# SyncE's queue in the last FFN part of a six-block decoder: stores of products wait for the load in flight

## What is computed

```python
x = act_qdq(x)
up = act_qdq(x @ lpbq_dequant(w_up).T)        # 256 -> 768
gate = act_qdq(x @ lpbq_dequant(w_gate).T)
sig = fixed_qdq_u16(jax.nn.sigmoid(gate))
gate = act_qdq(gate * sig)
o = act_qdq(gate * up)
return o @ lpbq_dequant(w_down).T             # 768 -> 256
```

## Time and profile before

| | us |
|---|---|
| median of 3 runs | 1373.13 |
| lowest, highest | 1371.76, 1376.19 |
| span of the profiled execution | 1374.7 |

### The profile page before, as it was taken

The page is one execution under the profiler, slowest core; times in us unless marked ns, Lnnn a source line. Parts: engine busy times, 40 slices in busy tenths (PEclk is TensorE's granted clock), DMA queues, the critical chain, the costliest instruction groups (busy, mean ns, idle before and its releaser), DMA issues.

```text
span 1374.7 us, 18473 instructions
## 1 busy us (share of the span) xinstructions
PE 1243.7 (90%) x7340; PEld 828.6 (60%) x7340; DVE 1048.2 (76%) x1966; ACT 517.7 (38%) x608; POOL 267.8 (19%) x194
## 2 busy tenths in 40 slices
PE   7899999997999999853779999999999999998976
PEld 4566666665644554321566776767768686766654
DVE  3578899986634789998564787969878797887777
ACT  1244334433534567587013323232322333231421
POOL 0011111112100000033100413204132141413242
PEclk9899999999999999976899999999999999999998
DMA  5001000102582045489322011100211000000000
GB/s 219 16 16 32 31 1 31 32 16 93 150 295 77 31 153 185 167 315 373 107 87 84 31 54 62 54 31 32 63 54 54 32 24 21 27 20 36 1 16 16
DMA packets 47829, 107.86 MB, mean 78 GB/s; under 512 B 10752, under 2 KB 31360, under 8 KB 44288
## 3 DMA queue, kind: packets, MB, share of 16 engines
q1 hardware_dynamic: 43584, 104.59, 21.7%
q10 hardware_dynamic: 4160, 2.10, 0.5%
HBM read 62.64 MB, written 44.04 MB: 78 GB/s over the span
## 4 chain that ended last, share of the span: by engine, by line
PE 74%; DVE 16%; DMA 3%; ACT 3%; issue 2%; POOL 1%; SPq 0%; POOLq 0%; ACTq 0%; DVEq 0%
PE ps L1357 8%; PE ps L1420 7%; PE ps L1236 6%; PE ps L1067 6%; PE ps L1118 4%; PE ps L817 4%; PE ps L1393 3%; PE ps L1302 3%; PE ps L965 2%; PE ps L890 2%; PE ps L1326 2%; PE ps L1337 2%; PE ps L1467 2%; DMA arena<-up_scratch 2%; PE ps L908 2%
## 5 line engine op out<-in xcount | busy, mean ns | idle before, releaser
L1420 PE MATMUL ps<-arena 128*128 128x256 f32 x512 | 120.1, 389 | 5.8 <-ACT arena L1892 5.8
L1357 PE MATMUL ps<-arena 128*128 128x512 f32 x256 | 117.6, 598 | 0.0
L1420 PEld LDWEIGHTS ps<-arena 128*128 128x128 f32 x512 | 98.6, 195 | 27.9 <-ACT arena L1892 9.9
L2535 DVE TENSOR_TENSOR arena<-ps,arena 128x2048 f32<-128x2048 f32 x32 | 73.3, 2292 | 38.1 <-PE ps L1302 37.9
L1938 POOL TENSOR_TENSOR arena<-arena 128x4 f32<-128x4 f32 x44 | 45.5, 1038 | 282.0 <-DVE arena L2124 282.0
L1998 POOL TENSOR_TENSOR arena<-arena 128x16 f32<-128x16 f32 x32 | 92.2, 2916 | 32.5 <-DVE arena L2564 32.5
L1236 PE MATMUL ps<-arena 128*128 128x256 f32 x384 | 88.2, 386 | 5.2 <-DVE arena L2456 5.2
L1067 PE MATMUL ps<-arena 128*128 128x512 f32 x192 | 83.8, 593 | 1.2 <-ACT arena L1620 1.2
L1118 PE MATMUL ps<-arena 128*128 128x512 f32 x192 | 84.4, 594 | 0.0
L1236 PEld LDWEIGHTS ps<-arena 128*128 128x128 f32 x384 | 73.0, 194 | 16.5 <-issue 7.0
L1357 PEld LDWEIGHTS ps<-arena 128*128 128x128 f32 x256 | 46.2, 190 | 48.7 <-issue 45.1
(11 more groups left out here) (311 smaller groups left out, 2651.9 us busy)
## 6 DMA issues: line engine op xcount, KB each, us to landing
v_scratch<-arena SPq DMA_DIRECT2D x7, 1536.0 KB, 12.9
arena<-v_scratch SPq DMA_DIRECT2D x7, 1536.0 KB, 6.8
up_scratch<-arena SPq DMA_DIRECT2D x6, 1536.0 KB, 6.0
arena<-up_scratch SPq DMA_DIRECT2D x6, 1536.0 KB, 12.6
vw_scratch<-arena SPq DMA_DIRECT2D x32, 256.0 KB, 3.8
arena<-x_scratch SPq DMA_DIRECT2D x16, 512.0 KB, 4.7
arena<-vw_scratch SPq DMA_DIRECT2D x8, 1024.0 KB
arena<-x SPq DMA_DIRECT2D x8, 512.0 KB, 5.7
```

Source lines behind the costliest of these rows:

```text
L1357: last = mm(flat(p % 2), w["cos_wq"][:, k, p * P:(p + 1) * P], xt4[:, k], start=k == 0, stop=k == NC - 1)
L1420: last = mm(flat(2)[:, C:2 * C], cos_pt[:, p], cos_vw[:, par, p], start=p == 0, stop=p == NP - 1)
L2535: v.tensor_tensor(met_s[:, n % 2].rearrange("p r t h n -> p (r t h) n"), flat(3, 4).rearrange("p (h n) -> p h n", n=P), w["causal"].unsque ...
```

## The change

A new helper on SP waits until the load of batch q has landed. It is put ahead of the stores of products 0 to 4. `load_up(4)` now stands ahead of `store_v(1)`, and `store_vw(15)` ahead of `store_v(2)`. No engine computes anything else or in another order, and the transfers are the same in number and size.

```diff
+            def up_landed(q):
+                wait_moved(sp, "up_loaded", Batch(q), q % 2, 2)
+
             load_up(2)
             store_vw(13)
             load_up(3)
+            up_landed(3)
             store_v(0)
             store_vw(14)
+            load_up(4)
+            up_landed(4)
             store_v(1)
-            load_up(4)
             load_up(5)
+            store_vw(15)
+            up_landed(5)
             store_v(2)
-            store_vw(15)
             load_up(6)
+            up_landed(6)
             store_v(3)
             load_up(7)
+            up_landed(7)
             store_v(4)
             store_v(5)
             store_v(6)
```

## The result

| | median, us | lowest, highest | runs |
|---|---|---|---|
| before | 1372.62 | 1369.85, 1377.73 | 19 |
| changed | 1378.11 | 1375.36, 1381.27 | 19 |

The changed kernel is slower. The ratio to before is 1.0033, with a 95% interval of 1.0022 to 1.0044, which is 3.0 to 6.0 us. The forecast was + 2.8 us and a time of 1375.9 within 1371.0 to 1381.0. The direction was right, and the time is in the range, but the size was a half to two thirds of what was measured. The outcome lies on the edge between "within 0.3%", to which I gave 0.68, and "slower by over 0.3%", to which I gave 0.29. The ratios in this document leave out three later runs of the kernel before, at 1494 to 2589 us.

What follows compares the result with a forecast made beforehand. Transfers, DVE and ACT were taken as nearly full, with the chain through load 6. Gaps at the gates, partly filled, and an earlier load 3 put load 6 2.8 us later: 1373.13 + 2.8 = 1375.9 us, range 1371.0 to 1381.0.

Steps and rivals of the forecast that it cites:

- What bounds, and the chain: From 600 to 630 us transfers, DVE and ACT are nearly full; the waits run through loads 4 and 6.
- The gates bind, and the queue runs dry: At SP's new waits, stores are held until a load lands and the queue empties, adding 2.4 us at loads 3 to 5.
- The landing of load 6: On SP's queue, load 6 lands at 632.6 us in place of 629.8, 2.8 us later.
- The two plain rounds: From load 4 to load 5 and on to load 6: a store and a load by bytes plus 2.4 us, 10.4 each.
- the first term: Issue of load 2 to landing of load 3: 9.3 us of bytes plus 2.4 us, landing at 600.1.
- The round with side store 14: From load 3 to load 4, with stores 0 and 14 ahead of load 4, which lands at 611.8 us.
- The long-gap rival: At the gates each restart of the queue costs 3.8 us, as the first did; + 4.1 to + 8.4 us, chance 0.25.
- The short gaps: At the gates the queue restarts in under 2.0 us; - 3.7 to + 1.2 us, chance 0.20.
- The estimate by the Trainium skill: On SP's queue, 2.0 us fixed per transfer and 436 GB/s put load 6 at 627.7 us and the time at 1371.0.
- ACT and load 4: On ACT, the 2.07 us wait for load 4 goes, since ACT is free at 612.6 us and the load has landed.
- From load 6 to the scale: ACT's 9.3 us of work follows load 6, DVE idles some 6 us, and the scale is ready at 660.3, 2.8 later.
- The tail: Store 6 lands at 661.3 us, 1.0 behind the scale, just covered; as rival setting the end, 1379.7 us, chance 0.04.

Runs made afterwards that it cites:

- covered gates: The changed kernel's order without the gate at load 3, the next load issued ahead of each gate at loads 4 to 7; ratio to before 0.9989.
- second run: The changed kernel run once more, with nothing altered; ratio to the kernel before 1.0034.
- gates 3 to 5: The changed kernel without the gates at loads 6 and 7; ratio to the kernel before 1.0046.
- gate 3 alone: The changed kernel's order of transfers with only the gate at load 3; ratio to the kernel before 1.0021.
- the two experiments: Changed kernel with side store 14 ahead of the gate at load 3, ratio 1.0032; and with side stores 13 to 15 at a quarter of their rows, 1.0023.
- the order without gates: The changed kernel with its new order of transfers on SP but without the five gates; ratio to the kernel before 0.9996.

## Why the prediction was right in direction and short in size

**What bounds, and the chain.** Right. The chain went through load 6, and with gates 6 and 7 away nothing changed, so what is behind load 6 wasn't on it.

**The gates bind, and the queue runs dry.** Right: stores of products were issued at 598.2, 611.7, 622.4, 632.6 and 642.9, and the covered gates show that it is the dry queue that costs.

**The landing of load 6** was put 44.2 us after the issue of load 2 (632.6 - 588.4) and came after 46.8 and 46.4. By its terms, with what the profiles of the changed kernel, its second run, gates 3 to 5 and (up to load 4) gate 3 alone measured:

| term | forecast | measured |
|---|---|---|
| issue of load 2 to landing of load 3 | 11.7 | 12.4, 13.3, 13.0, 13.4 |
| load 3 to load 4 | 11.7 | 13.6, 12.2, 12.2, 13.5 |
| load 4 to load 5 | 10.4 | 10.6, 10.8, 10.5 |
| load 5 to load 6 | 10.4 | 10.2, 10.1, 10.9 |

The two plain rounds of a store and a load were right: 4.0 + 4.0 + 2.4, against 10.5 on average. (That the 2.4 are there whatever the size isn't borne out: the 128 KB stores of y have 1.4. The sum uses it for 1536 KB only.) The step that failed is the first term. I had taken the 3.8 us over the bytes of load 3 for an effect of store 0 behind it, and forecast 2.4 once that store was held back, a gain of 1.4. With the gate, load 3 landed after 13.0 us on average. In the six lists in which store 0 followed it at once it landed after 12.6 to 14.5 us, 13.5 on average (13.1 in the kernel before, from which I had worked). So the gain was about 0.4, inside the spread of either group, in place of 1.4, and load 3 came 1.3 us later than forecast. What the 3.7 us over its bytes are stays open.

The round with side store 14 was short by 1.2 more, of which the two experiments explain a part. Slices of the changed kernel show a part too. The gate at load 3 opened at 598.2, and this is the rate behind it, GB/s last:

```profile
603.00:604.00 1.00, 0.00 (x0) 0.00 (x0) 1.00 (x1) 1.00 (x1) 1.00 (x1) 0.69 0.97 233
604.00:605.00 1.00, 0.00 (x0) 0.00 (x0) 1.00 (x1) 1.00 (x1) 0.92 (x2) 0.50 1.00 264
605.00:606.00 1.00, 0.00 (x0) 0.00 (x0) 1.00 (x1) 0.71 (x1) 1.00 (x1) 0.50 1.31 240
606.00:607.00 1.00, 0.00 (x0) 0.00 (x0) 0.96 (x3) 0.50 (x1) 1.00 (x1) 0.50 0.71 197
```

Against 394 GB/s these four lose 642 KB, worth 1.6 us. At the same place of the next round two slices have 224 and 270, which is 0.7 us. My sentence that SP issues a transfer in 0.3 us doesn't hold for side store 14 either: its two halves took SP 3.70 us, and load 4 was issued only at 602.36, though ACT had rounded batch 2 at 600.23. No run separates the two.

The long-gap rival took the 3.8 at every restart. It was right for load 3, and the plain rounds, which it would put at 11.8, refute it for the others. My sign for it, over 11 us from one load's landing to the next, was badly chosen: my own sum had 11.7 from load 3 to load 4. The short gaps, 2.0 and less, make a plain round 10.0 at most, and the six took 10.1 to 10.9; they miss the average by 0.5 us, but the shortest round by only 0.1. The note for them that stores land sooner than loads holds for those to `up_scratch`, 6.0 us against the 6.4 of the lone load, and not for those of products, 12.9. The estimate by the Trainium skill ("DMA: Bandwidth & Descriptors", section "Anatomy of one DMA") would have a plain round at 3.6 + 3.6 + 2.0 = 9.2 us, which no round reached, and load 6 earlier than before, which it wasn't.

**ACT and load 4.** I had written that ACT would be free for load 4 after 24.2 us (612.6 - 588.4) and find it landed since 23.4. The wait went, but not by this. Load 4 landed after 26.0 us, about as late as before (26.2), and ACT began to round it 611.97 - 585.76 = 26.2 us after the issue of load 2, just as before. Its list itself had come late, since `copy_vw(15)` waited for side store 14, which now stood behind the gate, and `copy_keys(0)` waited 2.57 us for PE (0.98 before):

```profile
606.50 1.02 ACT L1697 ACTIVATE arena<-ps 128x1024 f32<-128x1024 f32 x1 [0.79 <-DMA vw_scratch<-arena]
...
611.97 2.86 ACT L1765 ACTIVATE arena<-arena 128x3072 int16<-128x3072 f32 x1
```

In the second run, with gate 3 alone and with gates 3 to 5 the wait of `copy_vw(15)` is 1.9 to 2.7 us. The wait for PE isn't the gates' doing: it is 2.49 us in the order without gates. That this sign came true is luck, and it moved nothing, since load 6 is what the chain waits for. Two signs missed a little: loads 4, 6 and 7 landed 9.4 to 9.9 us after their issue, where I had 10 to 12, and ACT waited 1.14 us for load 7, where I had at least 1.5.

**From load 6 to the scale.** Right: the scale followed load 6 by 659.94 - 632.58 = 27.4 us, and by 657.28 - 629.8 = 27.5 before. DVE's wait was forecast at some 6 us and is 6.34.

**Load 7.** Forecast 11.7 us after load 6, with 1.3 for a store of keys; it took 10.3 and 10.2. The first store of keys was issued at 629.04, 3.5 us ahead of the landing of load 6 and not behind it; it cost nothing I can see. Since load 7 had room to spare, it didn't matter.

**The tail.** Store 6 was put at 72.9 us after load 2 and landed after 71.2, 3.0 us before the scale, so x rows were loaded without a wait. My sum put it 1.0 behind the scale; the margin was larger because the scale came 2.3 us later than forecast and the store 1.7 earlier.

**The chances.** The sum of the unknowns was put at + 1.2 to + 4.1 for the likeliest case. What was measured, + 3.0 to + 6.0, is the upper end of that and the lower end of the long gaps (+ 4.1 to + 8.4, to which I gave 0.25). The middle values, + 4.5 by the ratio and + 5.3 by the stretch, lie among the long gaps, though not by their mechanism. So the range held because it had room for a start that the sum had too short.

## What to carry to other kernels

When transfers are the bound, judge a change of the queue by bytes moved in the stretch and by when the load on the chain lands, and not by the time from issue to landing: here that fell by a half for stores while the kernel got slower. To favour loads, put them ahead of the stores in the list and keep another transfer in the queue at all times; here a wait for a landing with nothing queued behind it cost 2.7 to 3.8 us alone and 5.9 us for three in a row, and with another load queued behind it under 1 us. The gates behind the last transfer on which the chain depends were free.

## What the runs showed that I had not expected

The time lost at a gate is not one gap, and it looks different from gate to gate. These are slices of 1 us of the changed kernel (columns: busy time of PE, PEld, DVE, ACT, POOL, then clock, share of the transfer engines, GB/s). The gates opened at 598.2, 611.7, 622.4, 632.6 and 642.9.

```profile
597.00:598.00 1.00, 1.00 (x5) 0.23 (x3) 1.00 (x1) 1.00 (x2) 0.00 (x0) 1.00 0.09 37
598.00:599.00 1.00, 1.00 (x9) 0.65 (x8) 1.00 (x1) 1.00 (x1) 0.00 (x0) 1.00 0.06 16
...
610.00:611.00 1.00, 1.00 (x2) 0.33 (x1) 1.00 (x1) 1.00 (x1) 0.00 (x0) 0.50 0.35 147
611.00:612.00 1.00, 1.00 (x2) 0.33 (x1) 0.38 (x2) 1.00 (x2) 0.44 (x1) 0.50 0.00 0
612.00:613.00 1.00, 1.00 (x3) 0.47 (x2) 0.88 (x1) 1.00 (x2) 1.00 (x1) 0.50 0.36 137
...
622.00:623.00 1.00, 0.00 (x0) 0.00 (x0) 1.00 (x1) 0.59 (x1) 1.00 (x1) 0.50 0.91 320
...
637.00:638.00 1.00, 0.00 (x0) 0.00 (x0) 0.00 (x0) 1.00 (x1) 0.00 (x0) 1.00 0.99 215
...
642.00:643.00 1.00, 0.00 (x0) 0.00 (x0) 1.00 (x1) 0.09 (x1) 0.00 (x0) 0.50 0.96 295
```

At the gates of loads 3 and 4, with nothing of SP's or ACT's queued behind the load, the transfers all but stop: 37 and 16 GB/s, then 147, 0 and 137. That is the empty gap of the forecast. From the third gate on something else is in flight: the halves of `store_vw(15)` at load 5, a store of keys on ACT's queue at loads 6 and 7. There the rate only falls, to 320 GB/s at 622 and 295 at 642. A second fall comes some 5 us behind a gate, where the store ends and the load takes over: 224 GB/s at 616, 215 at 637. In it the engines' share stays near 1, so that column shows the gaps at the first two gates and not this loss. The model of 2.4 us without bytes gave the right length of a round and a part of its shape, and no run here tells why the change from a store to a load costs.

The second is how far two executions differ outside the change. These are the stretches before load 2 was issued, of the kernel before and of the changed one, with the same instructions in both:

```profile
0.00:588.41 588.41, 545.45 (x2797) 327.98 (x2797) 436.63 (x717) 259.97 (x296) 55.20 (x44) 0.97 0.26 90
```

```profile
0.00:585.76 585.76, 541.43 (x2797) 323.91 (x2797) 436.26 (x717) 259.81 (x296) 55.13 (x44) 0.98 0.26 91
```

The same 2797 matmuls took 545.4 us in one and 541.4 in the other, at a mean granted clock of 0.97 and 0.98. That alone is 2.7 us of span, half of the effect under study, and a like amount lies behind the stretch. It hid the whole change between the two profiled spans.
